# Token shifts by copies and DMA, the root in nine steps, gates behind their pairs, and new engine orders

## The reference

```python
for i in range(DEPTH):     # 6
    x = attn_layer(shift_tokens(x), Wqkv[i], q_scale[i], k_scale[i], Wo[i]) + x
    x = ffn_layer(shift_tokens(x), ln_g[i], ln_b[i], W1[i], b1[i], W2[i], b2[i]) + x

def shift_tokens(t):       # features 64..127 come from the token before
    a, s = jnp.split(t, 2, -1)
    s = jnp.pad(s, ((0, 0), (1, 0), (0, 0)))[:, :-1]
    return jnp.concatenate([a, s], -1)

def l2norm(t):             # on q and k, 16 heads of 64
    return t / jnp.maximum(jnp.linalg.norm(t, axis=-1, keepdims=True), 1e-12)
```

## Time and profile before

| | |
|---|---|
| median of 3 runs | 1876.19 us (1872.53 to 1881.08) |
| the profiled execution | 1868.75 us |
| its span, first to last instruction | 1867.0 us |
| first attention branch | 0 to 280.40 us |
| 24 pairs, counted from the first `xt_low` of each | 280.40 to 1801 us |
| remainder and gates | 1801 to 1867.0 us |

### The profile page before, as it was taken

How to read it: one execution, slowest core, us unless ns; L and a number is a source line. 1 busy time by engine, 2 the same in 40 slices (tenths; PEclk the granted TensorE clock), 3 DMA queues, 4 the chain that set the end, 5 groups by cost and what they waited for, 6 DMA issues and landing times. The chain is left out here.

```text
span 1867.0 us, 66200 instructions
## 1 busy us (share of the span) xinstructions
PE 1732.8 (93%) x26984; PEld 1428.9 (77%) x26985; DVE 1472.2 (79%) x2952; ACT 1404.0 (75%) x2772; POOL 1479.4 (79%) x1830
## 2 busy tenths in 40 slices
PE   6999967899999999999999999999999999999985
PEld 4788755777778888787887787877778877888773
DVE  5878847778977888888879787888888798889752
ACT  3777744678877888878877877888788878788862
POOL 3777757779888887988888879789888888898860
PEclk9999988999999999999999999999999999999998
DMA  4000011111121111111110211112111101110100
GB/s 140 1 1 1 1 36 34 31 44 32 31 68 44 33 43 32 58 44 42 44 32 22 68 44 43 31 33 67 40 37 44 32 22 41 38 50 22 37 27 23
DMA packets 45485, 70.67 MB, mean 38 GB/s; under 512 B 15476, under 2 KB 28928, under 8 KB 45184
## 3 DMA queue, kind: packets, MB, share of 16 engines
q1 hardware_dynamic: 43712, 64.34, 11.8%
q10 hardware_dynamic: 1472, 2.10, 0.3%
HBM read 21.33 MB, written 1.05 MB: 12 GB/s over the span
## 5 line engine op out<-in xcount | busy, mean ns | idle before, releaser
L1087 POOL TENSOR_TENSOR ra<-ra,rb 128x512 f32<-128x512 f32 x384 | 492.3, 1288 | 116.7 <-DVE rb L1083 111.6
L1132 POOL TENSOR_TENSOR qn<-ra,rs 128x512 f32<-128x512 f32 x384 | 401.3, 1058 | 7.2 <-POOL rs L1125 0.8
L1062 DVE TENSOR_REDUCE ss<-sq 128x8 f32<-128x512 f32 x384 | 260.4, 678 | 91.2 <-ACT sq L1051 91.2
L1214 POOL TENSOR_TENSOR sp<-sp,rl 128x512 f32<-128x512 f32 x192 | 200.0, 1046 | 61.7 <-DVE rl L1209 61.0
L1201 ACT ACTIVATE sp<-sp 128x512 f32<-128x512 f32 x192 | 121.7, 634 | 38.5 <-DVE sp L1196 38.1
L1205 DVE TENSOR_REDUCE sm<-sp 128x8 f32<-128x512 f32 x192 | 128.6, 670 | 15.5 <-ACT sp L1201 13.0
L1179 PE MATMUL pP<-kT,qT 64*32 64x64 f32 x4608 | 106.9, 226 | 2.8 <-issue 2.2
L1179 PEld LDWEIGHTS pP<-kT,qT 64*32 64x32 f32 x4608 | 93.8, 105 | 16.3 <-ACT kT L1152 11.0
L489 POOL TENSOR_TENSOR ra<-ra,rb 128x512 f32<-128x512 f32 x64 | 81.5, 1288 | 29.6 <-DVE rb L485 29.6
L1190 DVE TENSOR_REDUCE mx<-pS 128x8 f32<-128x512 f32 x48 | 32.9, 685 | 91.2 <-PE pP L1179 91.2
L1083 DVE TENSOR_TENSOR rb<-pQ,rope 128x512 f32<-128x512 f32 x144 | 97.9, 680 | 2.9 <-POOL ra L1087 2.9
(11 more groups left out here) (355 smaller groups left out, 6194.3 us busy)
## 6 DMA issues: line engine op xcount, KB each, us to landing
vs<-v SPq DMA_DIRECT2D x96, 384.0 KB, 3.3
wqkvA<-in_L_ffn_Wqkv SPq DMA_DIRECT2D x18, 512.0 KB, 5.6
vs<-v SPq DMA_DIRECT2D x96, 64.0 KB, 3.0
woB<-in_L_ffn_Wo SPq DMA_DIRECT2D x6, 512.0 KB, 4.2
w<-in_L_ffn_W SPq DMA_DIRECT2D x6, 341.0 KB, 2.9
out<-x SPq DMA_DIRECT2D x4, 256.0 KB, 2.3
x<-in_L_attn_x SPq DMA_DIRECT2D x1, 768.0 KB, 8.1
w<-in_L_ffn_W SPq DMA_DIRECT2D x12, 64.0 KB
```

Of the source, the lines that this page charges most:

```text
L1062: e.tensor_reduce(ss[:, j, :], sq[:, j % 2, :].rearrange("p (h d) -> p h d", d=DB), AX.X, ALU.add).then_inc(b_ss.sem, 1)
L1087: e.tensor_tensor(ra[:, j, :], ra[:, j, :], rb[:, j % 2, :], ALU.add).then_inc(b_ad.sem, 1)
L1132: e.tensor_tensor(qn[:, j % 4, :].rearrange("p (h d) -> p h d", d=DB), ra[:, j, :].rearrange("p (h d) -> p h d", d=DB), rs[:, c % 2, 8 * j ...
L1214: e.tensor_tensor(y, y, rl[:, u, :].unsqueeze(2).to_broadcast([P, 8, 64]), ALU.mult).then_inc(b_pn.sem, 1)
```

## The change

- `xt_turn` transposes the tiles unshifted (two transposes); `shifted` gives `xt_high` and `xt_low` two pieces each: the lower 64 partitions as they are, the upper 64 from one column to the left. Column 0 of the upper part is zeroed once.
- `l_shift` is now three DMAs on SyncE's queue, from `xr` straight into `fx` one partition further (one of 127 partitions x 4 tiles x 64 floats, two of one row). It waits for the pair's `out_add` and for the previous `l_norm`. `l_second` is gone; `l_first` is on ScalarE instead of GpSimd. SyncE's order takes `l_shift` between the moves of values.
- The inverse root takes nine steps (NORM = 9): the bit trick, then one polynomial of degree four in scalar_tensor_tensor steps. GpSimd does n = 0 to 4, VectorE 5 to 8.
- `finish` of pair q is called after the second pair behind it (`leave`, DONE = 2) instead of behind everything.
- The four orders and the tables of PSUM banks are new. In all four, turns 0 to 7 and both scores of a pair's second batch stand in the next pair (before, turns 0 to 3 and scores 0 stood in the own one). `l_stats` and `l_moments` move from the end of the pair before to the start of the pair that has the FFN: VectorE's pair now begins `rotate_cos(c-1, 7)`, `l_stats`, `xt_low(c)`, `rotate_sin(c-1, 7)`, `l_moments`, and ends `square_sum(c+1, 7)`, `out_add(c-1)`, four `norm_step`. TensorE's ends `proj(c+1, 8)`, `proj(c+1, 9)`, `out_proj(c-1, 0)`, `turn_p(c, 1)`, `out_proj(c-1, 1)`, `turn_p(c, 2)`, `turn_p(c, 3)`, `values(c, 0)` to `values(c, 7)`, `proj(c+1, 10)`, `proj(c+1, 11)`.

```diff
-NORM = 12
-ROOM = (1024.0 / 27.0) ** 2
+NORM, FIT = 9, 5
+SERIES = (1.0, -0.49999832, 0.37500061, -0.3139403, 0.27406215)
+ROOM = 1.0 / SERIES[4] ** 2
+HORNER = [x / SERIES[4] for x in SERIES[3::-1]]
...
-OUT_BANK = [6, 6]
-SHIFT_BANK, LTURN_BANK, Y_BANK = 7, 3, 6
-GATE_BANK = [3, 2, 0]
-A_BANK = [5, 4, 2]
+OUT_BANK = [6, 7]
+LTURN_BANK, Y_BANK = 4, 1
+GATE_BANK = [0, 2, 2]
+A_BANK = [0, 3, 5]
...
-            lo, hi = slice(0, HALF), slice(HALF, M)
-            xc = xr[:, (c % B) * NT:(c % B + 1) * NT, :]
             for t in range(NT):
-                e.matmul(o[lo, t * P:(t + 1) * P], xc[:, t, lo], ident, start=True, stop=True)
-            e.matmul(o[hi, 0:P], xc[:, 0, hi], down, start=True, stop=True)
-            e.matmul(o[hi, P:T], xc[:, 1, hi], down, start=True, stop=False, skip_group_check=True)
-            e.matmul(o[hi, P:T], xc[:, 0, hi], wrap, start=False, stop=True, skip_group_check=True)\
-             .then_inc(b_xt.sem, 1)
+                i = flip(e, o, t, xr[:, (c % B) * NT + t, :])
+            i.then_inc(b_xt.sem, 1)
+        def shifted(c, x_):
+            o = banks[XT_BANK[c % 2]]
+            return ((x_[0:HALF, c % 2, :], o[0:HALF, 0:T]), (x_[HALF:M, c % 2, 1:T], o[HALF:M, 0:T - 1]))
         def xt_high(e, l, c):
             it = l * B + c
             e.wait_ge(b_xt.sem, b_xt.at(it))
             e.wait_ge(b_pj.sem, b_pj.at(it - 2, NCH - 1))
-            e.copy(xsh[:, c % 2, :], banks[XT_BANK[c % 2]][:, 0:T]).then_inc(b_xh.sem, 1)
+            for dst, o in shifted(c, xsh):
+                i = e.copy(dst, o)
+            i.then_inc(b_xh.sem, 1)
         def xt_low(e, l, c):
             it = l * B + c
             e.wait_ge(b_xh.sem, b_xh.at(it))
-            e.tensor_tensor(xsl[:, c % 2, :], banks[XT_BANK[c % 2]][:, 0:T], xsh[:, c % 2, :].bitcast(F32),
-                            ALU.subtract).then_inc(b_xs.sem, 1)
+            for (dst, o), (h, _) in zip(shifted(c, xsl), shifted(c, xsh)):
+                i = e.tensor_tensor(dst, o, h.bitcast(F32), ALU.subtract)
+            i.then_inc(b_xs.sem, 1)
...
-            elif n in (2, 8):
+            elif n == 2:
                 e.tensor_tensor(t, y, x_, ALU.mult).then_inc(b_rs.sem, 1)
-            elif n in (3, 9):
+            elif n == 3:
                 e.tensor_tensor(t, t, y, ALU.mult).then_inc(b_rs.sem, 1)
             elif n == 4:
-                e.tensor_scalar(p, t, -10.0 / 3.0, None, ALU.add).then_inc(b_rs.sem, 1)
-            elif n == 5:
-                e.tensor_tensor(t, t, p, ALU.mult).then_inc(b_rs.sem, 1)
-            elif n == 6:
-                e.tensor_scalar(t, t, 5.0, None, ALU.add).then_inc(b_rs.sem, 1)
-            elif n == 7:
-                e.tensor_tensor(y, y, t, ALU.mult).then_inc(b_rs.sem, 1)
-            elif n == 10:
-                e.tensor_scalar(t, t, -1.0, 64.0 / 3.0, ALU.mult, ALU.add).then_inc(b_rs.sem, 1)
+                e.tensor_scalar(t, t, -1.0, None, ALU.add).then_inc(b_rs.sem, 1)
+            elif n == FIT:
+                e.scalar_tensor_tensor(p, t, HORNER[0], t, ALU.add, ALU.mult).then_inc(b_rs.sem, 1)
+            elif n < NORM - 1:
+                e.scalar_tensor_tensor(p, p, HORNER[n - FIT], t, ALU.add, ALU.mult).then_inc(b_rs.sem, 1)
             else:
                 e.wait_ge(b_qn.sem, b_qn.at(it - 2, QK - 1))
-                e.tensor_tensor(rs[:, c % 2, :], t, y, ALU.mult).then_inc(b_rs.sem, 1)
+                e.scalar_tensor_tensor(rs[:, c % 2, :], p, HORNER[n - FIT], y, ALU.add, ALU.mult).then_inc(b_rs.sem, 1)
...
         def l_shift(e, l, q):
+            it = l * FP + q
             e.wait_ge(b_wx.sem, b_wx.at(l * B + 2 * q + 1))
-            o = banks[SHIFT_BANK]
-            e.matmul(o[:, 0:FT * HALF], down, xr[:, tiles(q), HALF:M], start=True, stop=False, skip_group_check=True)
-            o = o[:, 0:FT * HALF].rearrange("p (b t m) -> p b t m", t=NT, m=HALF)
-            e.matmul(o[:, :, 1, :], wrap, xr[:, tiles(q), HALF:M].rearrange("p (b t) m -> p b t m", t=NT)[:, :, 0, :],
-                     start=False, stop=True, skip_group_check=True).then_inc(f_sh.sem, 1)
+            e.sem_inc(e_hold.sem, 1)
+            e.wait_ge(f_ln.sem, f_ln.at(it - 1))
+            e.sem_inc(e_hold.sem, 1)
+            k = (q % FP) * FT
+            e.dma_start(fx[1:P, :, HALF:M], xr[0:P - 1, k:k + FT, HALF:M]).then_inc(f_xs.sem, 16)
+            for b in range(FT // NT):
+                e.dma_start(fx[0:1, b * NT + 1, HALF:M], xr[P - 1:P, k + b * NT, HALF:M]).then_inc(f_xs.sem, 16)
         def l_first(e, l, q):
             it = l * FP + q
             e.wait_ge(b_wx.sem, b_wx.at(l * B + 2 * q + 1))
-            e.sem_inc(e_hold.sem, 1)
             e.wait_ge(f_ln.sem, f_ln.at(it - 1))
-            e.sem_inc(e_hold.sem, 1)
-            e.tensor_copy(fx[:, :, 0:HALF], xr[:, tiles(q), 0:HALF]).then_inc(f_xa.sem, 1)
-        def l_second(e, l, q):
-            it = l * FP + q
-            e.wait_ge(f_sh.sem, f_sh.at(it))
-            e.wait_ge(f_ln.sem, f_ln.at(it - 1))
-            e.copy(fx[:, :, HALF:M], banks[SHIFT_BANK][:, 0:FT * HALF].rearrange("p (t m) -> p t m", m=HALF))\
-             .then_inc(f_xs.sem, 1)
+            e.copy(fx[:, :, 0:HALF], xr[:, tiles(q), 0:HALF]).then_inc(f_xa.sem, 1)
...
+        def leave(e, q):
+            if 0 <= q < FP:
+                finish(e, q)
...
             e.memset(gT[64:P, 2, :], 1.0)
+            for y in (xsh, xsl):
+                e.memset(y[HALF:M, :, 0:1].bitcast(F32), 0.0)
...
-            stream(e, pair_dve)
-            remainder(e, pair_dve)
-            for q in range(FP):
-                finish(e, q)
+            stream(e, pair_dve, lambda p: leave(e, p - DONE))
+            remainder(e, pair_dve, lambda p: leave(e, p - DONE))
...
+                if l > 0:
+                    l_shift(e, l - 1, 3)
                 move_values(e, l, 1, 0)
```

More of the change, by code:

```diff
@@ L1480, in pair_pe @@
             if on(p - 1):
-                out_proj(e, l, c - 2, 1)
+                e.wait_ge(b_tc.sem, b_tc.at(l * B + c - 1, 7))
+                turn_p(e, l, c - 1, 0)
+            if on(p - 2):
+                e.wait_ge(f_G.sem, f_G.at(l * FP + p - 2, 0))
+            if on(p):
+                proj(e, l, c, 8)
+            if on(p - 1):
+                scores(e, l, c - 1, 1)
+            if on(p):
+                e.wait_ge(b_ab.sem, b_ab.at(l * B + c, 4))
+                proj(e, l, c, 9)
+            if on(p - 1):
+                e.wait_ge(b_pc.sem, b_pc.at(l * B + c - 1, 0))
+                turn_p(e, l, c - 1, 1)
+            if on(p):
+                e.wait_ge(b_ab.sem, b_ab.at(l * B + c, 5))
+            if on(p - 1) and not on(p):
+                e.wait_ge(b_tc.sem, b_tc.at(l * B + c - 1, 6))
+            if on(p - 1):
+                out_proj(e, l, c - 2, 0)
                 e.wait_ge(b_pc.sem, b_pc.at(l * B + c - 1, 1))
@@ L1485, in pair_pe @@
             if on(p):
-                e.wait_ge(b_ab.sem, b_ab.at(l * B + c, 3))
+                e.wait_ge(b_ab.sem, b_ab.at(l * B + c, 6))
+            if on(p - 2) and not on(p):
+                e.wait_ge(f_G.sem, f_G.at(l * FP + p - 2, 0))
             if on(p - 1):
@@ L1672, in pair_act @@
+            if on(p - 2):
+                gelu(e, l, p - 2, 0)
+                gelu(e, l, p - 2, 1)
+            if on(p - 1):
+                turn_copy(e, l, c - 1, 6)
+            if on(p):
+                square(e, l, c, 4)
+                e.wait_ge(b_ab.sem, b_ab.at(l * B + c, 3))
+            if on(p - 1) and not on(p):
+                e.wait_ge(b_tc.sem, b_tc.at(l * B + c - 1, 4))
+            if on(p - 1):
                 mask(e, l, c - 1, 2)
-                turn_copy(e, l, c - 1, 6)
@@ L1797, in pair_dve @@
             c = 2 * p
+            if on(p - 1):
+                rotate_cos(e, l, c - 1, 7)
+            if on(p - 2):
+                l_stats(e, l, p - 2)
             if on(p):
@@ L1800, in pair_dve @@
             if on(p - 1):
-                row_sum(e, l, c - 1, 1)
-                row_inverse(e, l, c - 1, 1)
+                rotate_sin(e, l, c - 1, 7)
+            if on(p - 1) and last(p - 1):
+                scaled_rope(e, l + (p - 1) // FP + 1)
+            if on(p - 2):
+                l_moments(e, l, p - 2)
             if on(p):
@@ new lines, in pair_dve @@
+            if on(p - 2):
+                gated(e, l, p - 2, 2)
+            if on(p):
+                square_sum(e, l, c + 1, 2)
+                rotate_cos(e, l, c + 1, 2)
+            if on(p) and last(p):
+                split_low(e, l + 1, 0, 1)
+            if on(p):
+                rotate_sin(e, l, c + 1, 2)
+                square_sum(e, l, c + 1, 3)
+                rotate_cos(e, l, c + 1, 3)
+                row_max(e, l, c, 0)
+                less_max(e, l, c, 0)
+                rotate_sin(e, l, c + 1, 3)
+                row_max(e, l, c, 1)
+                row_sum(e, l, c, 0)
+                less_max(e, l, c, 1)
+                square_sum(e, l, c + 1, 4)
+                rotate_cos(e, l, c + 1, 4)
```

(24 more changed lines are left out.)

824 lines of the change are left out of this document (402 added, 422 removed).

## The result

| | kernel before | changed kernel |
|---|---|---|
| median, us (runs) | 1874.36 (4) | 2027.67 (4) |
| span of the profiled execution, us | 1867.0 | 2024.3 |
| mean granted TensorE clock | 0.983 | 0.94 |

The ratio is 1.0815, 95% interval [1.0777, 1.0853]. The change makes the kernel slower by 153 us where the forecast was 50 us faster. Two things have to be explained: a loss of about 155 us, and a gain of about 50 that did not come.

A forecast was written before the change was run, and what follows sets the result against it. The prediction took TensorE's work to bound a plain pair: -42.2 us there, -7 at the start, +3 in the drain, -3.9 for the last gates sum to -50.1, giving 1818.6, or 1826 us as median; range 1795 to 1863.

## What to carry to other kernels

Before a transfer is costed from another's landing time, look at the counts of its slowest dimension on both: a count like 127 left a single DMA engine here, and cutting it in two pieces costs one more issue. Before a tuned loop is credited with what is taken from its busiest engine, ask what else would be late next in each queue; a short added operation on another engine, or on that engine, measures it in one run. And where a small edit of a matmul-dense stream moves the time by tens of microseconds, look at the idle time without a releaser: shift the stream by some idle instructions and measure again before believing any difference of a few per cent.

## What the runs showed that I had not expected

- TensorE stalls up to 3 us for its next block of 256 instructions, mostly where the last one was used up in under 3.3 us; 138 of 140 such stalls end 1.2 to 1.6 us after a 16.4 KB packet of the instruction queue. 64 idle instructions at the start moved this kernel from 1871 to 1942 us.
- A copy of 127 partitions from SBUF to SBUF runs at 17 GB/s (0.08 of sixteen engines), the same rows as 112 and 15 partitions at 105 (0.52).
- 4.7 us of idle time on TensorE drops its clock from 1.00 to 0.50; the stretch of 6 us behind it is granted 0.64, and over the kernel that costs 48 us beside 109 of idle time.
- VectorE's first operation after GpSimd's part of the root took 1.28 us, as long as the GpSimd operation that ran beside it, and 0.22 in a kernel where none did.
